# Splitting the tree weights on ScalarE and GpSimd instead of on VectorE

## The reference, cut to what matters

```python
# layer 1, feed-forward: each token goes to the best of 16 experts, at most 320 tokens each
x = x + _L1_ffn_ref(_layernorm(x), Wg, W1, b1, W2, b2)
# layer 2, feed-forward: three trees (q, k, v) choose a leaf, each leaf is a small MLP
hidden_all = relu(einsum('nd,ldh->lnh', xf, w1) + b1[:, None, :])
hidden = hidden_all * sel.T[:, :, None]
out = einsum('lnh,lho->no', hidden, w2) + sel @ b2
```

## Time and profile before

| what | value |
|---|---|
| runs | 1868.61, 1865.9, 1867.78 us; median 1867.78 us |
| span of the profiled execution, first to last instruction | 1867.0 us |
| PE busy | 1470.1 us (79%) |
| DVE busy | 1136.3 us (61%) |
| ACT busy | 617.3 us (33%) |
| POOL busy | 267.5 us (14%) |
| the 32 indirect DMAs of the scatter (L1504) | 42.9 us busy on POOL |

### The profile page before, as it was taken

The page is one execution under the profiler, slowest core; times in us unless marked ns, Lnnn a source line. Parts: engine busy times, 40 slices in busy tenths (PEclk is TensorE's granted clock), DMA queues, the critical chain, the costliest instruction groups (busy, mean ns, idle before and its releaser), DMA issues. The chain is left out here.

```text
span 1867.0 us, 26853 instructions
## 1 busy us (share of the span) xinstructions
PE 1470.1 (79%) x7749; PEld 1059.4 (57%) x7749; DVE 1136.3 (61%) x3732; ACT 617.3 (33%) x1055; POOL 267.5 (14%) x237
## 2 busy tenths in 40 slices
PE   3999977999967652206806998799999999879982
PEld 1666766989944442104504777466666666557771
DVE  5777664566648855731256886445555455478868
ACT  1444403444432210002204554233333333345541
POOL 1212100101001000271273220000000000022202
PEclk8999987999985555557857999799999999989995
DMA  6000000000000040004310000000000000000001
GB/s 211 1 0 0 1 0 1 1 1 0 1 1 1 0 150 0 3 38 127 99 37 5 1 0 1 1 1 1 1 1 0 0 1 1 1 1 0 0 1 46
DMA packets 38579, 34.21 MB, mean 18 GB/s; under 512 B 8672, under 2 KB 35552, under 8 KB 38112
## 3 DMA queue, kind: packets, MB, share of 16 engines
q1 hardware_dynamic: 35168, 26.78, 4.6%
q0 software_dynamic: 3328, 6.43, 1.0%
HBM read 24.14 MB, written 9.44 MB: 18 GB/s over the span
## 5 line engine op out<-in xcount | busy, mean ns | idle before, releaser
L484 POOL TENSOR_TENSOR mha_kbd<-KT,w_ctx 128x1024 f32<-128x1024 f32 x48 | 91.3, 1901 | 810.0 <-SPq L97 513.3
L1983 DVE SCALAR_TENSOR_TENSOR tree_hl<-tree_pH,tree_hh 128x512 fp32r<-128x512 f32 x192 | 132.3, 689 | 122.4 <-ACT tree_hh L1881 121.6
L392 PE MATMUL mha_pS<-mha_kbd,mha_qT 128*128 128x512 f32 x384 | 203.0, 612 | 4.3 <-ACT mha_qT L450 3.4
L425 PEld LDWEIGHTS mha_pO<-VB,mha_PT 128*128 128x128 f32 x1536 | 183.6, 193 | 10.8 <-issue 8.7
L425 PE MATMUL mha_pO<-VB,mha_PT 128*128 (+1 forms) x1536 | 178.7, 259 | 0.0
L1881 ACT ACTIVATE tree_hh<-tree_pH 128x512 fp32r<-128x512 f32 x192 | 114.6, 597 | 177.3 <-PE tree_pH L1784 177.3
L518 DVE TENSOR_REDUCE mha_nm<-mha_pS 128x8 f32<-128x512 f32 x192 | 131.5, 685 | 42.6 <-PE mha_pS L396 24.0
L521 DVE TENSOR_TENSOR mha_Z<-mha_pS,mha_nm 128x512 f32<-128x512 f32 x192 | 132.8, 692 | 19.3
L462 ACT ACTIVATE mha_PT<-mha_pT 128x1024 f32<-128x1024 f32 x96 | 98.3, 1024 | 136.8 <-PE mha_pT L407 136.6
L457 ACT ACTIVATE mha_PR<-mha_Z 128x1024 f32<-128x1024 f32 x96 | 101.5, 1057 | 85.4 <-DVE mha_Z L521 85.4
L407 PEld LDWEIGHTS mha_pT<-w_ctx,mha_PR 128*128 128x128 f32 x768 | 87.4, 141 | 38.4 <-issue 38.2
(11 more groups left out here) (421 smaller groups left out, 2828.9 us busy)
## 6 DMA issues: line engine op xcount, KB each, us to landing
w_tree_full<-in_tree_full_dram SPq DMA_DIRECT2D x1, 4224.0 KB, 13.9
exp_W<-in_L_W_dram SPq DMA_DIRECT2D x32, 128.0 KB, 2.3
slots_in<-route_zero SPq DMA_DIRECT2D x40, 64.0 KB, 1.9
w_rot<-in_rot_dram SPq DMA_DIRECT2D x1, 2307.0 KB, 8.7
X<-in_x_dram SPq DMA_DIRECT2D x8, 256.0 KB, 6.2
exp_xe<-slots_in SPq DMA_DIRECT2D x16, 128.0 KB, 2.9
slots_out<-exp_ye POOLq DMA_DIRECT2D x16, 128.0 KB, 2.8
out_dram<-X SPq DMA_DIRECT2D x8, 256.0 KB, 2.3
```

What stands on the lines that cost most here:

```text
L392: ins = pe.matmul(pS[:, n, :], qT[u][:, P * v:P * v + P], kbd[u][:, 8 * n:8 * n + 8, :], start=True, stop=not key_mask)
L425: ins = pe.matmul(pOv[:, c, :], PT[v][:, P * c:P * c + P], VB[:, a.b(-2), c, :], start=True, stop=True)
L484: pool.tensor_tensor(kbd[u][:], kb, bmask.unsqueeze(2).to_broadcast([P, H, SK]), ALU.mult).then_inc(s["kbd"], 1)
L1983: dve.scalar_tensor_tensor(hl[k % 2][:], pH[k % 2][:], 0.0, hh[k % 2][:], ALU.max, ALU.subtract).then_inc(s["lo"], 1)
```

## The change

`split_trees` returns two functions in place of issuing on VectorE. ScalarE runs its part right after the exponential L1402: two casts of 128 x 3072 (the high parts), two roundings of the bias tables to bf16 (`t1`), and later, when GpSimd has the rest, the second rounding (`t2`) and a multiplication of `t1` by a column of `part`, for each table. GpSimd runs its part at the beginning of its list, ahead of the wait for the slot numbers: two subtractions of 128 x 3072 and, for each table, four operations with two inputs and two with one input and a column as factor. Several of them write over what they read (`w(name)` and `t2`, `t1`). Seven semaphores tie the two engines and GpSimd's own steps together. VectorE's 18 operations are gone.

```diff
@@ route_top1
+        split_act, split_pool = split_trees(core, st)
...
             act.wait_ge(s["dx"], 1)
             act.activation(ex[:], ex[:], ACT.Exp).then_inc(s["ex"], 1)
+            split_act(act)
...
             dve.tensor_tensor(slots[:], sm[:], mx[:], ALU.add).then_inc(s["sl"], 1)
-            split_trees(core, st, dve)
...
         def _(pool):
+            split_pool(pool)
             pool.wait_ge(s["sl"], 1)
@@ split_trees, before
-        link(dve.tensor_copy(hi[:], full))
-        dve.tensor_tensor(lo[:], full, hi[:], ALU.subtract)
...
-        link(dve.tensor_copy(t1[q, :], w(name)))
-        link(dve.tensor_tensor(r[q, :], w(name), t1[q, :], ALU.subtract))
-        link(dve.tensor_copy(t2[q, :], r[q, :]))
-        link(dve.tensor_tensor(r[q, :], r[q, :], t2[q, :], ALU.subtract))
-        link(dve.tensor_scalar(t1[q, :], t1[q, :], part(rows, 0), None, ALU.mult))
-        link(dve.scalar_tensor_tensor(t1[q, :], t2[q, :], part(rows, 1), t1[q, :], ALU.mult, ALU.add))
-        link(dve.scalar_tensor_tensor(out, r[q, :], part(rows, 2), t1[q, :], ALU.mult, ALU.add))
@@ split_trees, after
+    def on_scalar(act):
+        act.wait_ge(core.trees_loaded, 16)
+        for full, hi in ((w("w1"), core.w1h), (w("w2"), core.w2h)):
+            act.activation(hi[:], full, ACT.Copy).then_inc(s_high, 1)
+        for n, (name, rows) in enumerate(PARTS):
+            act.activation(t1[n][0:rows, :], w(name), ACT.Copy).then_inc(s_t1, 1)
+        for n, (name, rows) in enumerate(PARTS):
+            q = slice(0, rows)
+            act.wait_ge(s_r, n + 1)
+            act.activation(t2[n][q, :], w(name), ACT.Copy).then_inc(s_t2, 1)
+            act.activation(t1[n][q, :], t1[n][q, :], ACT.Copy, scale=part(rows, 0)).then_inc(s_m1, 1)
+
+    def on_pool(pool):
+        link = Chain(pool, s_own)
+        for n, (full, hi, lo) in enumerate(((w("w1"), core.w1h, core.w1l), (w("w2"), core.w2h, core.w2l))):
+            pool.wait_ge(s_high, n + 1)
+            pool.tensor_tensor(lo[:], full, hi[:], ALU.subtract)
+        for n, (name, rows) in enumerate(PARTS):
+            q = slice(0, rows)
+            pool.wait_ge(s_t1, n + 1)
+            pool.tensor_tensor(w(name), w(name), t1[n][q, :], ALU.subtract).then_inc(s_r, 1)
+            pool.wait_ge(s_t2, n + 1)
+            link(pool.tensor_tensor(w(name), w(name), t2[n][q, :], ALU.subtract))
+            link(pool.tensor_scalar(w(name), w(name), part(rows, 2), None, ALU.mult))
+            link(pool.tensor_scalar(t2[n][q, :], t2[n][q, :], part(rows, 1), None, ALU.mult))
+            pool.wait_ge(s_m1, n + 1)
+            link(pool.tensor_tensor(t1[n][q, :], t1[n][q, :], t2[n][q, :], ALU.add))
+            link(pool.tensor_tensor(core.mix[q, n, :], w(name), t1[n][q, :], ALU.add))
```

More of the change, by code:

```diff
@@ L1686, in tree_buffers, with split_trees @@
     core.mix = sb("mix", [P, 2, MIXC], BF16)
-def split_trees(core, st, dve):
+def split_trees(core, st):
     w = lambda n: core.w("tree_full", n)
[L1694 to L1698, removed]
-        link(dve.tensor_copy(hi[:], full))
-        dve.tensor_tensor(lo[:], full, hi[:], ALU.subtract)
-    part = lambda rows, i: core.w("tree", "part")[0:rows, i:i + 1]
-    for n, (name, rows) in enumerate((("mixqk", P), ("mixv", SELP))):
-        q = slice(0, rows)
-        out = core.mix[q, n, :]
-        link(dve.tensor_copy(t1[q, :], w(name)))
-        link(dve.tensor_tensor(r[q, :], w(name), t1[q, :], ALU.subtract))
-        link(dve.tensor_copy(t2[q, :], r[q, :]))
-        link(dve.tensor_tensor(r[q, :], r[q, :], t2[q, :], ALU.subtract))
-        link(dve.tensor_scalar(t1[q, :], t1[q, :], part(rows, 0), None, ALU.mult))
-        link(dve.scalar_tensor_tensor(t1[q, :], t2[q, :], part(rows, 1), t1[q, :], ALU.mult, ALU.add))
-        link(dve.scalar_tensor_tensor(out, r[q, :], part(rows, 2), t1[q, :], ALU.mult, ALU.add))
@@ new lines, in split_trees @@
+    t1 = [st.sb(f"t1{n}", [P, MIXC], BF16) for n in range(2)]
+    t2 = [st.sb(f"t2{n}", [P, MIXC], BF16) for n in range(2)]
+    s_high, s_t1, s_r, s_t2, s_m1, s_m2, s_own = (
+        st.sem(n) for n in ("split_high", "split_t1", "split_r", "split_t2", "split_m1", "split_m2", "split_own"))
+    part = lambda rows, i: core.w("tree", "part")[0:rows, i:i + 1]
+    PARTS = (("mixqk", P), ("mixv", SELP))
+    def on_scalar(act):
[9 more added lines that the diff above has]
+            act.activation(t1[n][q, :], t1[n][q, :], ACT.Copy, scale=part(rows, 0)).then_inc(s_m1, 1)
@@ L1714, in attention_trees @@
+    return on_scalar, on_pool
 def attention_trees(core):
```

## The result

| | before | after |
|---|---|---|
| median of 7 runs | 1868.61 us | 1877.68 us |
| range of the runs | 1865.54 to 1873.15 | 1876.4 to 1885.77 |
| ratio, 95% interval | | 1.0059 [1.004, 1.0077] |
| profiled execution: its time, its span | span 1867.0 | 1884.69, span 1883.0 |

The change makes the kernel slower by 0.6%, as forecast (1876 us). On a base of 1867 us the interval is 7.5 to 14.4 us.

A forecast was written before the change was run, and what follows sets the result against it. No engine was full: VectorE's dependent search steps, then GpSimd's indirect DMAs, bound the stage. Span 1867.0 - 11.75 (scatter) + 20.1 (VectorE stalls) = 1875.4 us, median 1876, range 1869 to 1885 us for 8 in 10.

The forecast's parts named there:

- The path: Routing stage: VectorE's search chain, then GpSimd's 32 indirect DMAs set the time; VectorE's split ends almost 28 us earlier.
- The gain: Scatter: without VectorE's split all indirect DMAs run at the quiet pace, 40.56 us instead of 52.31, gaining 11.75 us.
- The stalls: mechanism: Before and in the search: VectorE operations with two SBUF inputs wait for a running GpSimd operation's end; 20.1 us.
- the two orders at 691.9 us: Before the search: VectorE already reading, 10.35 us of stalls, or GpSimd first, all three operations hit, 13.0 us.
- The stalls: size: Before and in the search: 19.6 or 20.6 us by order, taken as 20.1, from GpSimd's durations per column.
- The one-input price: GpSimd's one-input operations of 1152 columns: 2.1 us each taken; the skill's figure gives an estimate of 1.0 us.
- The variant of the sum with these four operations hidden: Search: at 1.0 us each, GpSimd's one-input operations would fit into gaps, and the sum would lose 2 us.
- The sum: Whole kernel: span 1867.0 - 11.75 + 20.1 = 1875.4 us, median 1876 us, slower by 0.5%.
- Rival 1, full lock-out: Search: one-column operations are blocked too, adding 6 to 10 us; time 1884 us, chance 0.16.
- Rival 2, faster: Search and before: GpSimd waits for VectorE instead, no step is delayed; time 1856 us, chance 0.10.
- Rival 3: Before and in the search: stalls sum to only 8 to 15.5 us, about even; time 1868 us, chance 0.12.

The follow-up runs named there:

- e1_psum: The changed kernel with the search's 28 counts reading the gate weights from PSUM, without the copy to SBUF: 1869.62 us, 1.0018 of the kernel before.
- e4_before_psum: The kernel before the change, with the search's counts reading PSUM and without the copy to SBUF: 1867.94 us, ratio 1.001.
- e2_psum_late: The changed kernel with counts reading PSUM and GpSimd's split waiting until the gate weights are formed: 1853.36 us, 0.9935 of the kernel before.
- the repeat: The changed kernel timed once more, unaltered: 1878.02 us, 1.0067 of the kernel before.
- e3_late: The changed kernel with GpSimd's split waiting until the gate weights are formed, counts still reading SBUF: 1874.28 us, 1.0049 of the kernel before.
- e7_pieces: The changed kernel with each GpSimd operation of the split cut into 384-column pieces, counts from SBUF: 1859.84 us, 0.9964 of the kernel before.
- e5_dve_rest: The changed kernel with GpSimd's part issued on VectorE after the slot numbers, beside the scatter: 1862.12 us, 0.9978 of the kernel before.

## Why the prediction was right, step by step

- **The path.** Right. GpSimd's scatter, not VectorE's split, ended the stage, and the search is a chain in which each delay of VectorE counts in full: 14.1 + 9.4 us of stretched operations are 23.5, and the slot numbers came 23.6 us later.
- **The gain.** 11.75 us forecast, 11.5 measured; the first indirect DMA took 1.22 us instead of 0.97, the rest as forecast.
- **The stalls: mechanism.** Right, and shown: taking the second SBUF input away (e1_psum, with e4_before_psum as control) removes 9.4 us, keeping GpSimd away from the three operations before the search removes the other 14.1 (e2_psum_late). Of the two orders at 691.9 us the second came true: GpSimd started 0.08 us ahead of VectorE and all three operations were hit. In the search 11 counts were hit, as forecast; each of GpSimd's 14 operations held up one VectorE operation.
- **The stalls: size.** 20.1 us forecast (20.6 for that order), 23.6 measured: 14.1 instead of 13.0 before the search, 9.4 instead of 7.6 in it. The mis-sized terms are GpSimd's durations. In the search its four multiplications cost 4.6 us, not 2.0, and its seven operations with two inputs 4.9, not 5.6. The long subtractions take 6.7 us, not the 5.7 that `up_l` gave at 1.86 ns a column; the same operation in the same formats runs at 2.17 ns here, and no run says why. The one-input operations take 3.2 us unhindered, not 2.1. The two-input operations of 1152 columns take 2.36 us unhindered (e2_psum_late), in place or not, where 2.8 in place and 2.1 otherwise were forecast. No row has the 0.05 us from a count's end to GpSimd's start: taking the unhindered durations off GpSimd's ends (712.56 - 6.66 = 705.90, against 706.06), its work begins 0.16 us before the end of the operation it waits for. The Trainium skill's figure for two-input operations (GPSIMD Engine Reference, section Performance versus the Vector engine), about 2.6 cycles an element, gives an estimate of 6.66 us for 3072 columns at its 1.2 GHz; the measurement sides with it against the row that I took. For the 2048 columns of `up_l` itself that figure of the Trainium skill gives an estimate of 4.44 us, and the row has 3.81: it fits one of the two.
- **The one-input price.** The Trainium skill's 1.03 cycles an element (the same section), an estimate of 1.0 us for 1152 columns, doesn't hold for this multiplication: the rows of e1_psum and e2_psum_late say 3.2 us, in f32 and in bf16. The variant of the sum with these four operations hidden would have missed by more.
- **The sum.** By the stage, +8.35 us was forecast and +12.1 measured. That the median (1877.68) lies so near 1876 is partly luck: the two medians of 7 runs differ by 9.1 us, those of the repeat by 11.9.
- **Rival 1, full lock-out,** is refuted for one column by L1441 and L1442, at 0.27 and 0.20 us beside a running GpSimd operation; two columns were enough in the kernel before (last section). **Rival 2, faster,** is refuted: VectorE waited in all 14 stretched operations. **Rival 3** did not arise, but e1_psum shows how near it is: with the 9.4 us of the search gone, 0.2% remain.

## What to carry to other kernels

Before work is moved to an idle GpSimd, look at what VectorE does on the critical chain at that time: each operation with two SBUF inputs there can wait for the whole GpSimd instruction that runs, and the wait hides inside its duration. Some with one input can too: L926, 256 columns, took 3.33 us instead of 0.29. What kept its duration beside GpSimd here read PSUM, reduced one input or moved one column. Give the chain a PSUM source, start GpSimd where the chain has no such operation, or cut GpSimd's work into short instructions; of the 23.5 us the PSUM source took 9.4 away, the later start 14.1 more (alone only 3.7, as the search has such operations too), and the short instructions alone 17.8. An operation's price is to be taken from a row of its own kind and size, and where there is none the bounds should be as wide as 1 to 3 us for one column count.

## What the runs showed of the hardware that was not expected

- GpSimd's multiplication of 1152 columns by a column of factors takes 3.20 us, more than its subtraction of two inputs, 2.36 us. Here are both in e2_psum_late, where nothing hinders them (busy, mean ns):

```profile
L1717 POOL TENSOR_TENSOR w2l<-w_tree_full,w2h 128x3072 fp32r<-128x3072 f32 x1 | 6.7, 6655 | 0.0
L1724 POOL TENSOR_SCALAR w_tree_full<-w_tree_full,w_tree 128x1152 f32<-128x1152 f32 (+1 forms) x2 | 6.4, 3196 | 0.2
L1725 POOL TENSOR_SCALAR route_t<-route_t,w_tree 128x1152 bf16<-128x1152 bf16 (+1 forms) x2 | 6.4, 3194 | 0.2
L1723 POOL TENSOR_TENSOR w_tree_full<-w_tree_full,route_t 128x1152 f32<-128x1152 f32 (+1 forms) x2 | 4.7, 2362 | 2.5 <-ACT route_t L1710 2.5
```

- The two engines take turns: a count that waited goes before GpSimd's next instruction, which is then longer by its own wait, 0.44 us where it was issued at once (7.10 against 6.66 us) and 0.08 to 0.33 where it was issued later. No count waited for two GpSimd instructions, in the changed kernel, in e3_late or in e7_pieces.
- How few columns escape: VectorE's operations with one tensor input of 128x1 keep their duration beside GpSimd (L1441, L1442), one of 128x2 doesn't. In the kernel before L551 takes 0.17 us, and 0.33 or 0.34 where it starts well inside L484, which here ends at 177.75:

```profile
175.85 1.90 POOL L484 TENSOR_TENSOR mha_kbd<-KT,w_ctx 128x1024 f32<-128x1024 f32 x1 [7.50 <-PE mha_pS L396]
177.44 0.33 DVE L551 TENSOR_SCALAR MV<-mha_mv 128x2 f32 x1 [0.16 <-DVE mha_mv L549]
```

- An indirect DMA's issue on GpSimd waits for a VectorE operation with two SBUF inputs too: 3.37 us instead of 0.97 beside a 3.35 us subtraction, with no cast in sight (e5_dve_rest). The Trainium skill (SBUF — State Buffer, section Who interferes with whom) infers that such an operation leaves descriptor generation alone; for an indirect DMA these rows say otherwise.
